# A first held tile before the last sum over states, back-part stages at the end of a tile's turn, and a late round's pads in two pieces

## What is computed

```python
# Mamba part, per batch
dA  = exp(einsum('bld,dn->bldn', delta, A));  dBu = einsum('bld,bln,bld->bldn', delta, Bm, xc)
h = dA_t * h + dBu_t ;  y_t = einsum('bdn,bn->bd', h, C_t)      # lax.scan over 2048 steps
y = (ys + xc * D) * silu(z) ;  x1 = x1 + y @ out_w.T            # "out_proj"
normed = _ln(x1, n2_g, n2_b)
x1 = x1 + (silu(gate) * val) @ ffp_w.T + ffp_b                  # "ff_gate", "ff_val", "ff_out"
x = x + x1                                                       # "x_four"
# experts, on layernorm(x)
topk_w, topk_idx = top_k(xt @ Ws + bs, 2);  topk_w = softmax(topk_w)   # "route", "top", "choice", "rank"
h = silu(einsum('td,edf->tef', xt, Wg)) * einsum('td,edf->tef', xt, Wu)
y = einsum('tef,efd->ted', h, Wd);  out = einsum('ted,te->td', y, combine)
x = x + out
```

## Time and profile before

| | us |
|---|---|
| median of 3 runs | 898.7 (896.98 to 903.21) |
| the profiled execution | 898.42 |
| its span | 896.5 |
| busy: PE, DVE, POOL, ACT | 666.5, 726.3, 573.2, 504.6 |

### The profile page before, as it was taken

How to read it: one execution, slowest core, us unless ns; L and a number is a source line. 1 busy time by engine, 2 the same in 40 slices (tenths; PEclk the granted TensorE clock), 3 DMA queues, 4 the chain that set the end, 5 groups by cost and what they waited for, 6 DMA issues and landing times. The chain is left out here.

```text
span 896.5 us, 13066 instructions
## 1 busy us (share of the span) xinstructions
PE 666.5 (74%) x3706; PEld 481.6 (54%) x3706; DVE 726.3 (81%) x1128; ACT 504.6 (56%) x1092; POOL 573.2 (64%) x488
## 2 busy tenths in 40 slices
PE   4358578678768886797788768877884877898963
PEld 2134245445335534774477446744673556798963
DVE  1378779989998999979998999999999865474363
ACT  2547676766766576556756575557553663443421
POOL 1095556566856895789768985888669934345332
PEclk9679699889879977998799988988797889999997
DMA  6833133213312336542654255434642423457794
GB/s 179 248 113 114 47 94 118 79 65 108 119 48 90 106 100 185 152 127 86 186 162 118 90 171 155 125 106 132 173 150 80 129 63 99 135 160 216 204 311 130
DMA packets 95450, 118.24 MB, mean 132 GB/s; under 512 B 11351, under 2 KB 63395, under 8 KB 95363
## 3 DMA queue, kind: packets, MB, share of 16 engines
q1 hardware_dynamic: 90835, 108.02, 41.3%
q0 software_dynamic: 4544, 9.38, 2.9%
HBM read 105.37 MB, written 16.34 MB: 136 GB/s over the span
## 5 line engine op out<-in xcount | busy, mean ns | idle before, releaser
L695 POOL TENSOR_TENSOR inflow<-du,b_wide 128x1024 f32<-128x1024 f32 x128 | 316.2, 2473 | 170.6 <-DVE product L960 109.4
L950 DVE TENSOR_TENSOR_SCAN state<-decay,carry,inflow 128x512 f32<-128x512 f32 x192 | 235.0, 1265 | 6.2 <-ACT decay L814 5.8
L814 ACT ACTIVATE decay<-delta,a_neg 128x512 f32<-128x512 f32 x256 | 171.9, 690 | 104.6 <-DVE state L950 101.1
L722 POOL DMA_INDIRECT y_dram<-y_rows,x_rows x78 | 86.8, 1112 | 82.0 <-ACT y_rows L870 73.4
L960 DVE TENSOR_TENSOR product<-state,c_wide 128x1024 f32<-128x1024 f32 (+1 forms) x98 | 135.8, 1386 | 2.8 <-PE y L1150 1.7
L1150 PE MATMUL y<-ident,product 128*128 128x128 f32 x704 | 106.2, 297 | 41.9 <-DVE product L960 41.8
L1150 PEld LDWEIGHTS y<-ident,product 128*128 128x128 f32 x704 | 87.2, 153 | 79.9 <-DVE product L960 50.0
L1155 PE MATMUL y<-h_rows,ident 128*128 128x512 f32 x160 | 101.2, 755 | 33.6 <-ACT h_rows L779 33.6
L716 POOL DMA_INDIRECT row_dram<-m_tok,place x64 | 72.7, 1136 | 25.8 <-issue 19.8
L950 DVE TENSOR_TENSOR_SCAN state<-decay,inflow 128x512 f32<-128x512 f32 x64 | 74.8, 1212 | 9.2 <-ACT decay L814 6.6
L1106 PE MATMUL work_front<-u_t,w_tap 128*128 128x512 f32 x128 | 64.1, 628 | 6.0 <-ACT u_t L750 4.4
(11 more groups left out here) (210 smaller groups left out, 1285.1 us busy)
## 6 DMA issues: line engine op xcount, KB each, us to landing
b_wide<-bc_dram SPq DMA_DIRECT2D x128, 256.0 KB, 3.3
w_stage<-gate_up_dram SPq DMA_DIRECT2D x78, 344.0 KB
c_wide<-bc_dram SPq DMA_DIRECT2D x98, 256.0 KB, 3.5
x_rows<-row_dram SPq DMA_DIRECT2D x78, 65.0 KB, 3.6
x_tok<-in_x SPq DMA_DIRECT2D x8, 256.0 KB, 6.2
out<-x_tok SPq DMA_DIRECT2D x8, 256.0 KB, 4.6
inflow<-y_dram SPq DMA_DIRECT2D x6, 256.0 KB, 4.2
gate_up_dram<-in_Wg SPq DMA_DIRECT2D x1, 1376.0 KB, 8.9
```

What stands on the lines that cost most here:

```text
L695: e.tensor_tensor(inflow[:, key % 3], du[:, c % 2], b_wide[:, key % ROW_SLOTS:key % ROW_SLOTS + 1, :].to_broadcast([P, HALVES, CHUNK]), AL ...
L722: e.indirect_dma_start(y_dram, bass.IndirectOffsetOnAxis(x_rows[:, key % X_SLOTS, ID_AT:ROW].bitcast(u32), 0), y_rows[:, key % Y_SLOTS, :] ...
L814: e.activation(decay_bank[h][:], delta[:, c % 2, h, :], ACT.Exp, scale=a_neg[:, h, n:n + 1]).then_inc(S["decay"], 1)
L950: e.tensor_tensor_scan(state[:, key % STATE_SLOTS, h, :], decay_bank[h][:], inflow[:, key % 3, h, :], 0.0 if c % (SEQ // CHUNK) == 0 else ...
```

## The change

It touches `plan()` only. No instruction is added or taken away; the 2688 entries of the list are the same ones in another order. The first entry that differs comes after `carry` of the last unit.

1. `turn` lets a held job through in the last unit. So `x_turn` and `x_cols` of job 33 stand before `h_turn` of unit 127, its gate, tanh and up after `place` of chunk 6 and before `total` of unit 127. `moe_h` of job 33 stands before `y_gate` of chunk 7.
2. The tail loop begins at job 34 (`m + 1`). In each turn the steps of the back part that start on POOL, PE or ACT/DVE (`back[0]`, `back[1]`) and the piece of the list now stand at the end, behind the add, and the PE steps (`back[2]`) right behind the next turn's first half. `x_turn` of job 35 comes behind the first half of job 34.
3. `pads0` and `pads1` stand in two turns, in place of one.

By turns of the tail the back part of chunk 7 ends up later: `rank` of chunk 7 in turn 48 (46 before), `late0` at the end of turn 48 (47 before), `tag0` in turn 49 (47), its scatters in turns 50 to 58 (48 to 56), `load_x` of job 63 in turn 59 (57 before).

```diff
     def turn(m, now):
-        if now < len(UNITS) and JOBS[m][0] >= HELD_ROUND:
+        if now < len(UNITS) - 1 and JOBS[m][0] >= HELD_ROUND:
             return
@@ the loop over units
-        if moving:
+        if i == len(UNITS) - 1:
+            turn(m, i + TURN_LAG)
+        elif moving:
             put("moe_h", m)
             turn(m + 1, i)
@@
-        if not moving and ("x_turn", m) not in done and n in (SHARES_LAST if c == CHUNKS - 1 else SHARES):
+        if not moving and (("x_turn", m) not in done or i == len(UNITS) - 1) and n in (SHARES_LAST if c == CHUNKS - 1 else SHARES):
             free.append(i)
@@
-    tail = m + (("x_turn", m) in done)
+    tail = m
@@
-        return [[("late0", c)], [("pads0", c), ("pads1", c), ("late1", c)], [("late2", c)]]
+        return [[("late0", c)], [("pads0", c), ("late1", c)], [("pads1", c), ("late2", c)]]
@@
-    put_all(moving[:1 + SUB], *take_back(1))
+    put_all(moving[:1 + SUB])
+    put("moe_h", m)
     moving = [moving[1 + SUB:3 + SUB]] + [[step] for step in moving[3 + SUB:]]
-    now = first
-    for t in range(m, len(JOBS) + 2):
+    now, back = first, take_back(1)
+    put_all(*back[:2])
+    for t in range(m + 1, len(JOBS) + 2):
         for q in range(t, t + X_SLOTS):
             load(q, 0)
-        for q in (t, t + 1):
-            if q == t or q < len(JOBS) and JOBS[q][1]:
-                turn(q, len(UNITS) + TURN_LAG)
+        turn(t, len(UNITS) + TURN_LAG)
+        if t > m + 1 and t + 1 < len(JOBS) and JOBS[t + 1][1]:
+            turn(t + 1, len(UNITS) + TURN_LAG)
         first_half(t)
-        back = take_back(1)
-        put_all(*back)
-        if any(back) and not backs:
-            moving, listing, now = [[step] for step in moves(last)], late_list(last), last
-        if listing:
-            put_all(listing.pop(0))
-            if not listing:
-                listed.add(now)
-        if m <= t - 1 < len(JOBS):
+        if t == m + 1:
+            turn(t + 1, len(UNITS) + TURN_LAG)
+        put_all(back[2])
+        if m < t - 1 < len(JOBS):
             put("moe_h", t - 1)
@@ behind down, y_rows and add of t - 2
+        back = take_back(1)
+        put_all(*back[:2])
+        if any(back) and not backs:
+            moving, listing, now = [[step] for step in moves(last)], late_list(last), last
+        if listing:
+            put_all(listing.pop(0))
+            if not listing:
+                listed.add(now)
```

## The result

The changed kernel takes 893.29 us (median of 19 runs), the kernel before 898.84 (19 runs); the ratio of the two is 0.9945, with a 95% interval of 0.9925 to 0.9964, so 3.2 to 6.7 us are saved.

The account below looks back on a forecast made before the run. PE was taken to bound the tail's first 56 us (48.3 busy), with waits to cover. Transpose 64 7.5 us earlier, less 0.5, took 7.0 off 898.42, giving 891.4; with 0.3 for the median, forecast 891.5, range 887.5 to 897.5.

Parts of the forecast that it names:

- The first held tile: Before the last sum: job 33's transpose, gate and up fill PE's 1.66 us wait, gaining 1.34 us.
- Stages at the end of a turn: From the last sum to job 46's down: PE waits fall from 9.0 to 4.8 us, gain taken as 3.6.
- The named waits: PE waits expected to stay or arise between the last sum and job 46's down, 4.8 us in all.
- Pads: Tiles 54 to 56: pads in two pieces turn one 3.24 us wait into 1.0 and 2.3; tile 56 lands at 810.5.
- The half clock: After the 2.3 us wait at tile 56: PE's clock falls for a turn, charged at 1.67 us.
- Last scatter and transpose 64: Chunk 7's scatters: last issued at 821.4 us with the half clock; transpose 64 at about 829.7, 7.5 earlier.
- Behind transpose 64: Transpose 64 to the end: nothing is reordered, so the 59.3 us there are kept.
- my own test: Prediction is wrong if job 46's down ends after 797, or the stretch behind transpose 64 is not 59 us.
- R3: Tail, slower: PE's new short waits hold the clock at half, 1.67 us a turn, 901 with ten; chance 0.05.
- R1: Tail: the clock does not fall and the walk is exact, 9.8 us gained, about 889; chance 0.25.
- R2: Tile 56: late add and row load behind the pads take most back, gain 3.9, about 894.8; chance 0.2.

Follow-up runs that it names:

- after_again: The changed kernel, unaltered, run and traced again on chip B: 894.95 us, ratio 0.9947 to the kernel before.
- a_only: Kernel before with only job 33's transpose, gate and up ahead of the last sum, its gating unmoved: ratio 1.0016 on chip A, 0.9966 rerun (_2) on chip C.
- before_again: The kernel before, unaltered, traced again on chip B: 159.91 us from the start of the last two scans to the end.
- a_and_b: The changed kernel with all eight pads in one turn again: ratio 0.9965 to the kernel before, on chip A.
- b_only: Kernel before with only the back part's stages at the end of a turn: ratio 1.0030 on chip A, 1.0003 rerun on chip C.
- ahead41: The changed kernel with tile 41 also turned and copied one turn ahead: 891.76 us, ratio 0.9899 to the kernel before, on chip B.

## Why the prediction was right

**The first held tile.** Predicted: the last sum 0.1 later, job 33's matmuls done before it. Measured: mark 8.28 before, 8.39 after, and up of job 33 (its last group starts 1.15 before the sum) is done. That this is worth 1.34 by itself was wrong: alone, without its gating moved, it gave 0.3, with the lower clock behind it; beside the moved stages it gave 2.0 (60.46 to 58.47) on other chips, and 1.0 (60.65 to 59.66) on chip A.

**Stages at the end of a turn.** With the first tile: job 46's down to end 4.9 earlier. Its start went from mark 62.68 to 57.72, 4.96. The named waits: 1.0 before tile 39 (1.09 measured), 1.9 before gate of job 41 (1.56), 0.75 before `n_tok`'s transpose (0.32), 0.55 before `m_tok`'s (0.78), 0.1 before job 42 (0.57 before transpose 45). The sum is 4.3, and 4.3 it was in the forecast; the single terms were off by up to 0.5 and cancel, which is luck.

**Pads.** Predicted: waits of 1.0 and 2.3, tile 56 at 810.5 on the clock of before, mark 74.8. Measured: 1.63 and 1.58, mark 75.86. The sum of the waits, 3.2, is the predicted 3.3, though each was off by 0.6 to 0.7. The tile is 1.1 later than forecast: tile 54 was loaded at mark 63.05, as forecast (62.9), but SP came to the load of tile 56 only 9.5 us later (72.58), for which I had 9.1, and that load took 3.23 to land in place of 2.71.

**The half clock.** I charged 1.67 at the edge. In the first trace it did not come, in `after_again` it came and cost 2.9. The rule that I took from rows (falls after 2.32, not after 2.01) does not hold: 3.02 was followed by the full clock. So the 1.67 in the sum stands between the 0 of one trace and the 2.9 of the other.

**Last scatter and transpose 64.** Predicted 821.4 and 829.7 on the clock of before, marks 85.7 and 94.0; measured 85.20 and 93.38, and 87.62 and 95.77 in the second trace.

**Behind transpose 64.** Predicted 59.3 us to the end. The traces have 60.7 and 59.4 for the changed kernel, 60.0 for the second trace of before, and 58.6 to 61.1 for all other kernels that leave the merge alone. Nothing is seen to be gained or lost there beyond that spread. By the letter of my own test ("wrong if it is not 59 us") the first trace, 60.7, is off by 1.5: that much of the 8.1 gained at transpose 64 was gone at the end.

**The size.** 7.0 was forecast for the trace, 7.2 for the medians; 5.55 is the difference of the medians, 3.2 to 6.7 by the interval. The term that was mis-sized is the starting point of the last step, transpose 64 of the kernel before at 837.24, mark 101.51. That execution had lost about 2 us at tiles 61 and 64 to row loads that came late; in the second trace of before neither wait is there, and the mark is 99.90. From there to 95.77 it is 4.1, to 93.38 it is 6.5, where I had 7.5. One trace was taken for the kernel.

**A sentence that was wrong.** I wrote that nothing before 739 us can move. The edit moves nothing there, but executions differ by up to 10.8 us in that stretch.

**A sum that was wrong.** R3 says that ten turns at half the clock would give 901. Ten times 1.67 is 16.7, and on the forecast of 891.5 that is 908; no chance changes by it.

**The rivals.** R1's missing half clock came true in one trace of two, and 9.8 in none. R2 (the DMA chain takes most back): its mechanism is seen on chip A, where adds landed late, for kernels with one or two of the parts; the whole change was not run there. R3: in both runs of `a_only` a stretch of 4.8 us behind two short waits of 0.78 and 0.94 had a mean granted clock of 0.64 (below, `a_only_2`, columns as in the earlier trace rows), so the lower clock can follow short waits; the kernel before, with 1.66, 0.78 and 0.49 in the same place, kept 1.00, and so did the changed kernel in its first 66 us. The Trainium skill's "TensorE: Matmul & The Clock Gate", Part 1, says that the throttle follows activity; these rows agree in so far as the falls came behind idle stretches, but not each idle stretch brought one.

```profile
750.78:755.58 4.80, 4.80 (x30) 4.72 (x29) 2.45 (x8) 1.26 (x3) 2.98 (x4) 0.64 0.49 109
```

## What to carry to other kernels

Where several engines follow one written order, a lead that one edit wins is spent at the next queue that is full for a moment (here small transfers in a row on SP): look for that queue before adding up gains. The stages alone brought transpose 50 forward by 3.6 us and the end by 1 to 2; with the pads split as well the end came 5 to 7 earlier. Work out what a burst costs its queue and what a turn leaves free there. Two pieces of four moved the wait by a tile or two; four pieces of two, with a turn between, removed it at tiles 55 and 56 and brought 2.5 us of it back at tiles 59 to 62, since two turns left 1.3 us and a piece took 2.0. An experiment on a part should carry every line that belongs to the part: `a_only` left out the gating of its tile. Where the start of the edited stretch varies by more than the edit is worth, measure from an instant inside the trace, take two traces of the kernel before ahead of any sum, and trace it again on each chip where a variant runs.

## What the runs showed of the hardware

- The same kernel on two chips, one trace on each: `b_only` had a tail of 165.13 on one and 158.70 on the other. Issuing eight pads of 65 KB each from SP took between 5.9 (`before_again`) and 8.5 us (`a_and_b`).
- The granted clock after a wait of PE is not told by the wait's length: full after 3.02 us (`ahead41`), at the lower level after 2.68 (`after_again`), and 0.64 over 4.8 us after two waits of 0.78 and 0.94 (`a_only_2`). Nor is the cost: behind the wait for rows, transposes 54 to 56 took 5.75 to 5.94 us in the kernel before and 6.86 in `a_only_2`.
- The time from transpose 64 to the end lay between 58.6 and 61.1 us in the 13 traces with the old merge, while transpose 64 itself lay between marks 91.5 and 105.9; the DMA engines were at a share of 1.07 to 1.1 for some 20 us of it.
